# Routed rows loaded by transposing DMAs instead of TensorE transposes and ScalarE copies

## The reference

```python
logits = xt @ gate_w.T
scores = softmax(logits)
idx = top_k(scores + gate_b, 2)[1]           # two of eight experts for each token
cw  = sum(one_hot(idx, 8) * scores[idx], axis=1)
h1 = einsum('td,efd->etf', xt, w1) + b1[:, None, :]      # 256 columns: gate and linear interleaved
h3 = einsum('td,efd->etf', xt, w3) + b3[:, None, :]
a = swiglu(h1 * h3)                          # min/clip at 7, g * sigmoid(1.702 g) * (l + 1)
y = einsum('etf,edf->etd', a, w2) + b2[:, None, :]
routed = einsum('te,etd->td', cw, y)
out = routed + shared_expert(xt)
x = x + 0.5 * out
```

## Time and profile before

| What | Value |
|---|---|
| device time, three runs | 1515.95, 1521.43 and 1524.22 us (median 1521.43) |
| profiled execution: span from the first to the last instruction | 1515.8 us |
| profiled execution: its own device time | not recorded apart; the median run is 5.6 us above the span |
| granted TensorE clock, mean | 0.950 of full speed |
| DMA | 94.3 MB, mean 62 GB/s |

### The profile page before, as it was taken

How to read it: one execution, slowest core, us unless ns; L and a number is a source line. 1 busy time by engine, 2 the same in 40 slices (tenths; PEclk the granted TensorE clock), 3 DMA queues, 4 the chain that set the end, 5 groups by cost and what they waited for, 6 DMA issues and landing times.

```text
span 1515.8 us, 42570 instructions
## 1 busy us (share of the span) xinstructions
PE 1313.6 (87%) x15621; PEld 1012.9 (67%) x15621; DVE 1153.5 (76%) x3632; ACT 805.2 (53%) x1302; POOL 672.4 (44%) x727
## 2 busy tenths in 40 slices
PE   1566987798978889888898899999999999999998
PEld 0344765576766777666676777777876776767776
DVE  5888788779756698788898587767688778877775
ACT  0344655436534556453566456767666546546662
POOL 0056637785557357767678433221433335210100
PEclk9978999899989999999999999999999988989999
DMA  9002313332143214221333221121110010000000
GB/s 284 0 29 76 104 52 105 90 87 71 52 116 100 66 52 113 70 69 53 107 91 96 71 77 44 40 58 46 43 37 17 22 33 25 17 24 2 9 16 23
DMA packets 128044, 94.30 MB, mean 62 GB/s; under 512 B 15723, under 2 KB 119302, under 8 KB 127590
## 3 DMA queue, kind: packets, MB, share of 16 engines
q1 hardware_dynamic: 108038, 54.17, 12.3%
q0 software_dynamic: 16384, 33.59, 7.6%
q10 hardware_dynamic: 3424, 3.81, 0.8%
HBM read 45.90 MB, written 45.61 MB: 60 GB/s over the span
## 4 chain that ended last, share of the span: by engine, by line
PE 54%; DVE 25%; issue 7%; POOL 6%; ACT 5%; DMA 1%; SPq 0%; POOLq 0%; DVEq 0%; ACTq 0%
PE bank L668 9%; PE bank L725 4%; POOL rows L1605 3%; PE bank L682 3%; PE bank L661 3%; PE bank L702 2%; POOL y_in L1622 2%; PE bank L752 2%; PE bank L530 2%; PE sums L899 2%; PE bank L882 2%; PE sums L913 2%; PE bank L489 2%; DVE heads_store L940 2%; DVE heads_store L1020 1%
## 5 line engine op out<-in xcount | busy, mean ns | idle before, releaser
L1622 POOL DMA_INDIRECT y_in<-ys,r_result x256 | 273.5, 1069 | 120.9 <-issue 69.7
L1605 POOL DMA_INDIRECT rows<-store,r_slot x256 | 264.0, 1031 | 108.9 <-issue 75.8
L668 PE MATMUL bank<-u_xp_odd,w_hi 128*128 128x128 f16 x1216 | 128.6, 224 | 6.9 <-ACT u_xp_odd L1391 6.7
L668 PE MATMUL bank<-u_xp_even,w_hi 128*128 128x128 f16 x1216 | 126.8, 221 | 4.8 <-ACT u_xp_even L1391 4.7
L661 PE MATMUL bank<-r_member,by_expert 128*128 128x512 bf16 x304 | 118.0, 388 | 8.9 <-ACT u_linear_even L1471 3.1
L668 PEld LDWEIGHTS bank<-u_xp_odd,w_hi 128*128 x1216 | 96.5, 100 | 32.4 <-issue 12.0
L668 PE MATMUL bank<-u_xp_odd,w_lo 128*128 128x128 f16 x608 | 117.8, 223 | 0.0
L668 PE MATMUL bank<-u_xp_even,w_lo 128*128 128x128 f16 x608 | 115.7, 220 | 0.0
L668 PEld LDWEIGHTS bank<-u_xp_even,w_hi 128*128 x1216 | 95.1, 98 | 30.1 <-issue 9.2
L1416 ACT ACTIVATE heads_store<-bank,b3s,sc 128x512 f32<-128x512 f32 x64 | 49.4, 775 | 72.3 <-PE bank L530 72.1
L530 PE MATMUL bank<-heads_store,w_hi 128*128 128x512 f16 x256 | 81.8, 403 | 3.8 <-ACT u_linear_odd L1471 1.4
(11 more groups left out here) (348 smaller groups left out, 3797.8 us busy)
## 6 DMA issues: line engine op xcount, KB each, us to landing
u_rows<-rows SPq DMA_DIRECT2D x304, 64.0 KB
ys<-u_y_even SPq DMA_DIRECT2D x38, 256.0 KB
ys<-u_y_odd SPq DMA_DIRECT2D x38, 256.0 KB
x<-x_dram SPq DMA_DIRECT2D x16, 256.0 KB, 7.3
rows<-store,r_slot POOLq DMA_INDIRECT x256
y_in<-ys,r_result POOLq DMA_INDIRECT x256
out_dram<-x SPq DMA_DIRECT2D x16, 256.0 KB
rows<-blank SPq DMA_DIRECT2D x48, 64.0 KB, 1.5
```

The source lines that it names most:

```text
L668: ins = pe.matmul(B[:, of_block[j]], of_expert(wp, e, 2 * part + which), s.xp[:, xp, of_block[j]], start=False, stop=(n == 2 and j == PER_ ...
L1605: pool.indirect_dma_start(row_dram[g], bass.IndirectOffsetOnAxis(route.slot[g][:, i, t:t + 1].bitcast(U32), 0), rows[:, groups[g].first * ...
L1622: pool.indirect_dma_start(fetch.y[i][:, t, k, :], None, y_dram[g], bass.IndirectOffsetOnAxis(route.result[g][:, k, t0 + t:t0 + t + 1].bitc ...
```

## The change

The four loads of a unit become four transposing DMAs. Each reads a block of 128 rows x 256 float16 numbers from DRAM and writes it turned, as 128 partitions x 2 x 128 columns, straight into the layout that `project` reads. There are five buffers of this layout (`unit_xp`) in place of three of rows and two of turned rows. Step 0 of a unit does nothing any more on TensorE and ScalarE; the bank that it took from the rotation is not taken. `project` waits for the landing of its unit's four DMAs. SP may overwrite a buffer when the last projection of five units earlier is done. The two places that waited for the transposes of the last units of pass 0, before the DRAM rows are overwritten in pass 1, wait for the first projection's result instead. The lists of steps stay as they are.

```diff
+XP_BUFFERS = 5
-        rows_in = [sem(f"rows_in{i}") for i in range(3)]
+        rows_in = [sem(f"rows_in{i}") for i in range(XP_BUFFERS)]
-        unit_rows = [sb(f"u_rows{i}", [P, T, 2, D], F16) for i in range(3)]
+        unit_xp = [sb(f"u_xp{i}", [P, 2, N], F16) for i in range(XP_BUFFERS)]
         unit_lanes = [lane(name) for name in ("even", "odd")]
         for s in unit_lanes:
-            s.xp = sb("u_xp_" + s.name, [P, 2, N], F16)
...
             def experts(l, g, u, k):          # TensorE
                 use = (l, g, u)
-                if k == 0:
-                    turn_rows(use)
-                elif k == 1:
+                if k == 1:
...
-            def turn_rows(use):
-                l, g, u = use
-                s = unit_lanes[u % 2]
-                M = bank("units", "xp", *use)
-                on.wait_ge(rows_in[load_index(use) % 3], 16 * PER_UNIT * (load_index(use) // 3 + 1))
-                s.by_tensor.mark(split_turned(M, unit_rows[load_index(use) % 3]), "xp", *use)
-                ring.free_at(("units", "xp", *use), s.by_scalar, "xp", *use)
-
             def project(use, part):
-                s = unit_lanes[use[2] % 2]
+                s, i = unit_lanes[use[2] % 2], load_index(use)
+                xp_rows = unit_xp[i % XP_BUFFERS]
...
-                    on.wait_ge(*s.by_scalar.at("xp", *use))
+                    on.wait_ge(rows_in[i % XP_BUFFERS], 16 * PER_UNIT * (i // XP_BUFFERS + 1))
...
-                                            s.xp[:, xp, of_block[j]], start=False,
+                                            xp_rows[:, xp, of_block[j]], start=False,
...
             def experts(l, g, u, k):          # ScalarE
-                if k == 0:
-                    on.wait_ge(*s.by_tensor.at("xp", *use))
-                    split_copied(s, s.xp[:], ring["units", "xp", l, g, u], "xp", *use)
-                elif k == 1:
+                if k == 1:
...
-                        on.wait_ge(*unit_lanes[u % 2].by_tensor.at("xp", l - 1, g, u))
+                        on.wait_ge(*unit_lanes[u % 2].by_tensor.at("h", l - 1, g, u, 0, 0))
...
-                if i >= 3:
-                    on.wait_ge(*unit_lanes[(i - 3) % 2].by_tensor.at("xp", *unit_uses[i - 3]))
+                if i >= XP_BUFFERS:
+                    far = unit_uses[i - XP_BUFFERS]
+                    on.wait_ge(*unit_lanes[far[2] % 2].by_tensor.at("h", *far, 1, 1))
                 for j in range(PER_UNIT):
-                    sp.dma_start(unit_rows[i % 3][:, j:j + 1, :, :].rearrange("p s k d -> p s (k d)"),
-                                 block_of(row_dram[g], firsts[j])).then_inc(rows_in[i % 3], 16)
+                    sp.dma_start_transpose(unit_xp[i % XP_BUFFERS][:, :, of_block[j]],
+                                           block_rows(row_dram[g], firsts[j])).then_inc(rows_in[i % XP_BUFFERS], 16)
```

More of the change, by code:

```diff
@@ L81 @@
     scalar_tensor_tensor = tensor_reduce = reciprocal = bn_stats = bn_aggr = dma_start = emit
-    tensor_tensor_scan = indirect_dma_start = memset = wait_ge = then_inc = emit
+    tensor_tensor_scan = indirect_dma_start = dma_start_transpose = memset = wait_ge = then_inc = emit
 class Ring:
@@ L1643, in load_numbers, with block_rows @@
                 return list(values)
+            def block_rows(dram_rows, first):
+                return dram_rows[0:BLOCK, :] if first is None else dram_rows[bass.ds(first, BLOCK), :]
             def block_of(dram_rows, first):
-                picked = dram_rows[0:BLOCK, :] if first is None else dram_rows[bass.ds(first, BLOCK), :]
-                return picked.rearrange("(s p) c -> p s c", p=P)
+                return block_rows(dram_rows, first).rearrange("(s p) c -> p s c", p=P)
             def clear_ends(l, g):
```

## The result

The changed kernel takes 1541.1 us in the median of four runs (1529.7 to 1546.2) beside 1521.0 us for the kernel before: 1.3% slower, ratio 1.0129 with a 95% interval of 1.009 to 1.0168. Measured once more (six executions) it was 1551.3 beside 1519.4, ratio 1.0208 (1.017 to 1.0245). The time lies in the stated range, on the other side of what was forecast.

The account below looks back on a forecast made before the run. TensorE, busy 89% of the stretch with units, was taken to lead, not alone. 14.7 (transposes) + 3.2 (copies) + 0.8 (old group's last store) made 18.7 us less: 1503 us, range 1488 to 1555.

Parts of the forecast that it names:

- I take p = 0.6, near the lower end: SP's queue: p, the time by which one transposing load follows another, taken as 0.6 us between 0.52 and 1.86.
- threshold at 1.2: Row loads on SP: from p = 1.2 us on, late stores and rows were to cancel the gain.
- the transposing DMAs run one after another: Rival at group starts on SP's queue: p = 1.5 us, late stores hold POOL's fetches; 1531 to 1554 us, chance 0.33.
- the half that I let through: In the serial rival, 22.6 of 45.3 us of POOL's late fetches were counted, since several next-layer chunks are in work.
- TensorE's term, 14.7 us,: Stretch with units: removed transposes hold 16.6 us of the chain; 89%, TensorE's busy share, was to come through.
- the sign that I had named for a wrong chain: TensorE: busy time falls and idle time rises by as much, which would show the chain reading wrong.
- The copies' term, 3.2 us,: ScalarE's copies of turned rows: a third of their 9.5 us on the chain was to be gained; ends nothing and 9.5.
- The steady part and the buffers: Between group starts: loads hidden at p 0.6 and 1.5 us; with five buffers SP's 89.4 us of waits go.
- The first units: Group starts: first unit's rows there after 4.2 us, second's after 6.6 against 8.7 wanted; both covered.
- The 1.8 us for a landing: Group starts: landing time of a unit's rows, from 3.7 us until transposes began and 1.9 us for four loads.
- the rival's 5 us for a late second unit: Third group, serial rival: second unit's rows there after 13.8 us, 5.1 us late.
- my estimate of 2.6 us from two tiles: Row loads on SP: p if each load costs two 128x128 crossbar transposes of 1309 ns; the kernel would take some 1565 us.

## Why the prediction was wrong

**The step that failed** is "I take p = 0.6, near the lower end". The price p is 22.2 / 16 = 1.39 us with the table reads at a group start, 1.29 us from one issue of a unit to the next, of which the DMA itself holds SP for 1.17. The reason given, same bytes and contiguous rows, argued about the transfer, while the price is on the issuing engine, and of that the trace of before had no row. The bounds held it. An unknown price with a threshold at 1.2 between bounds of 0.5 and 1.86 should not have been put at 0.6 with a chance of one half.

**The rival** "the transposing DMAs run one after another" had the place right, the store of the old group's last unit behind 16 loads, and POOL without cover at 577 and 877 us. Its mechanism was wrong: SP itself is busy for the time by which the store is late, and plain DMAs that keep SP as long do the same (1553.6), so no draining on the DMA engines is needed to explain it. Its size, by its own formula with what was measured: lateness 13.4, 13.2, 11.4 and 9.2 us less the slack 8.3, 1.6, 0 and 0 leaves 37.3 us, where POOL's waits grew by 40.8 us, from 7.0 to 47.8. The changed kernel stands 32 us above the same kernel with plain loads by the ratios of the first runs, 1541.1 - 1503.2 = 37.9 by their medians, and 1551.3 - 1511.9 = 39.4 where both were measured side by side. So more of it comes through than the half that I let through; that is the second mis-sized term. But it is not waiting alone. Between the first two profiles, with the same 15013 matmuls, the span grows by 37.3 us, of which 26.8 are idle time of TensorE and 10.5 are busy time: the same matmuls take longer, at a granted clock of 0.922 instead of 0.937. That this 37.3 is also the figure of the formula is chance. In the second pair of profiles the span grows by 50.7 us, 36.0 of them idle and 14.7 busy.

**TensorE's term, 14.7 us,** measured nothing. The pieces of a chain that ended last are not a gain when they go, and 89% busy time was the wrong measure of what comes through. It went by the sign that I had named for a wrong chain: without the transposes TensorE's busy time falls by 22 to 24 us and its idle time rises by 22. That VectorE, with 25% of the chain, is what it meets next is argued, not shown. Part of the 34 us does not even leave the busy time, which falls by 16.4 us in the changed kernel where I expected 30 to 45. A lower granted clock goes with it, in the median 0.933 without the transposes and 0.946 with them, over twelve executions each; whether the clock takes the gain back or follows from the idling was not told apart.

**The copies' term, 3.2 us,** was too small. They carry the whole gain of 8 to 14 us (10.5 us in the run without copies and with transposes), around the upper of the ends that I gave, 0 and 9.5. That TensorE's wait for them, 11.4 us, is about as large fits; I had taken a third.

**The steady part and the buffers** came out about as said: TensorE waited 2.0 us for rows in all, and five buffers and SP's waits were worth nothing. *The first units* were covered less than I reckoned: at the third group the projection began 8.0 us after the first load (427.64 to 435.68), not 4.2, and TensorE waited 1.7 us for it. The 1.8 us for a landing was no measurement either: by the earlier trace rows TensorE's idle time before those transposes was ended by VectorE, not by the rows. One reading was wrong in my favour and against me at once. The projection at 437.81 us, which I took for the second unit's, is the first unit's second part. The second unit's own began here, in the kernel before and in the changed one (TensorE's timeline; start us, us):

```profile
442.81 0.60 PE L661 MATMUL bank<-r_member,by_expert 128*128 128x512 bf16 x1
```
```profile
435.68 0.28 PE L659 MATMUL bank<-u_xp,w_hi 128*128 128x128 f16 x2 [1.74 <-DMA u_xp<-rows]
...
443.98 0.63 PE L652 MATMUL bank<-r_member,by_expert 128*128 128x512 bf16 x1
```

It is wanted 13.7 us after the first load, not 8.7, and with p = 1.3 and my own 1.8 us for the landing its rows would be there after 8 x 1.3 + 1.8 = 12.2 us; TensorE began it at 443.98 without waiting for them. So the rival's 5 us for a late second unit were none: late rows play next to no part in the loss.

**The pages.** By the Trainium skill (Advanced Engine Details and Errata, X-Bar Transpose (TRN2)) transposing DMAs are as fast as regular ones. The kernels agree in time once the stores are elsewhere (1505.4 against 1504.9 us), where the transfers are hidden. The transfers themselves were somewhat dearer here. SP's DMA queue in these two runs, with plain and then with transposing loads (packets, MB, share of the 16 engines' span):

```profile
q1 hardware_dynamic: 67910, 34.24, 7.9%
```
```profile
q1 hardware_dynamic: 111686, 34.26, 9.3%
```

For the same bytes that is 119 and 139 us of each engine. And of the first unit of the third group the last load was issued at 431.55 and its rows were used at 435.68, 4.1 us later, where plain DMAs of 64 KB landed after 1.5. Of the issue, 1.17 against 0.33 us, the rule says nothing. The 1309 ns of VectorE: DVE Perf Modes (The three transpose paths) for 128x128 come near to the 1.29 us from issue to issue, but not as the price of a tile: 128x256 took 1.17 us and 64x256 took 1.16, so my estimate of 2.6 us from two tiles was as wrong as the 0.6. (The rival's 1565 us for it was scaled up in a straight line; the terms themselves, with half of the lateness, give some 1575.)

## What to carry to other kernels

A DMA has two prices: its transfer, which prefetching hides, and its issue, which delays everything behind it on the issuing engine. Before exchanging one kind of DMA for another, list what stands behind each burst of them in that engine's order, and who waits for it; put the transfer that somebody waits for ahead of the prefetches that nobody waits for yet, or on another engine that has room. Work taken off a busy engine is worth what its consumers wait for: here the copies between two engines paid, and the saving on the busiest engine, which the chain that ended last had priced higher, did not.

## What the hardware showed that was not expected

SP is held for 1.17 us by a transposing DMA of 128x256 float16 and for 1.16 us by one of 64x256. A plain DMA of 128 rows of 512 bytes holds it for 0.33 us, one of 64 rows for 0.47 us, more for half the bytes; those of 48 and 32 rows held it for 0.32. Cutting a plain load of 128 rows into two of 64 made the kernel 3% slower than with whole ones (ratios 1.0209 and 0.992 to the kernel before). For the same bytes the transposing loads made 43776 more packets, 144 for each load. ScalarE is held for 0.37 us by each store that it issues. And the same kernel before took 1799 us in one series of runs and 1517 to 1519 in the others, for a reason that no profile shows.
